# A recommender's cross-product tower on one core: tiles of 32 rows by 16 positions, lookups of four fields at once, and fifteen field pairs of the first layer multiplied out

## The reference, cut to what matters

```python
def _cin_layer(x0, xk, W, b):
    out = jnp.einsum('bhd,bmd,shm->bsd', xk, x0, W) + b[None, :, None]
    return jax.nn.relu(out)
e = jnp.stack([tbl_0[ids[:, 0]], ..., tbl_38[ids[:, 38]]], axis=1)   # (1024, 39, 16)
x1 = _cin_layer(e, e, W1, b1)        # W1 (128, 39, 39)
x2 = _cin_layer(e, x1, W2, b2)       # W2 (128, 128, 39)
z = jnp.concatenate([x1.sum(axis=-1), x2.sum(axis=-1)], axis=-1)
h = jnp.concatenate([z, dense_ctx], axis=1)
h = jnp.maximum(h @ W_top1 + b_top1, 0.0)
h = jnp.maximum(h @ W_top2 + b_top2, 0.0)
y = h @ W_top3
```

## Time and profile before

| | us |
|---|---|
| three runs | 1270.61, 1272.14, 1273.03 (median 1272.14) |
| the profiled execution | 1272.45 |
| its span, first to last instruction | 1270.7 |

### The profile page before, as it was taken

The page is one execution under the profiler, slowest core; times in us unless marked ns, Lnnn a source line. Parts: engine busy times, 40 slices in busy tenths (PEclk is TensorE's granted clock), DMA queues, the critical chain, the costliest instruction groups (busy, mean ns, idle before and its releaser), DMA issues.

```text
span 1270.7 us, 17332 instructions
## 1 busy us (share of the span) xinstructions
PE 1190.3 (94%) x4794; PEld 880.8 (69%) x4794; DVE 980.5 (77%) x3635; ACT 616.4 (49%) x1897; POOL 847.7 (67%) x788
## 2 busy tenths in 40 slices
PE   1279999999999999999999999999999999999996
PEld 0147777777777777777777667777777777776774
DVE  0118888888888888888888667888988888887695
ACT  2154555555545555555545444555555555554440
POOL 6788787777777777777778456877777544553450
PEclk9999999999999999999999999999999999999997
DMA  5000000000000000000000000000000000000000
GB/s 170 6 5 3 4 3 4 3 4 3 4 3 3 3 3 4 3 3 3 3 3 3 3 3 3 3 3 3 3 3 3 1 1 1 1 1 1 1 1 1
DMA packets 12837, 8.91 MB, mean 7 GB/s; under 512 B 6645, under 2 KB 12010, under 8 KB 12611
## 3 DMA queue, kind: packets, MB, share of 16 engines
q0 software_dynamic: 9984, 2.58, 2.4%
q1 hardware_dynamic: 2755, 5.22, 1.3%
HBM read 7.78 MB, written 0.00 MB: 6 GB/s over the span
## 4 chain that ended last, share of the span: by engine, by line
PE 82%; DVE 11%; POOL 3%; ACT 2%; issue 2%; DMA 0%; ACTq 0%; DVEq 0%
PE ps L592 20%; PE ps L594 19%; PE ps L593 19%; PE ps L572 15%; DVE acc L507 11%; PE ps L563 3%; POOL e L283 3%; PE ps L621 3%; ACT fy L374 1%; PE ps L551 1%; PE ps L668 0%; ACT z L396 0%; PE ps L659 0%; PE ps L658 0%; DMA e<-in_tbl,ids_sb 0%
## 5 line engine op out<-in xcount | busy, mean ns | idle before, releaser
L507 DVE SCALAR_TENSOR_TENSOR acc<-ps,e,acc 128x128 f32<-128x128 f32 x3200 | 854.1, 343 | 182.7 <-PE ps L594 179.3
L592 PE MATMUL ps<-w2h,x1h 128*128 128x512 f32 (+1 forms) x1280 | 591.6, 462 | 17.2 <-DVE acc L507 14.1
L292 POOL TENSOR_TENSOR fy<-fy 128x512 f32<-128x512 f32 (+1 forms) x256 | 401.3, 1568 | 284.2 <-ACT fy L374 264.7
L374 ACT ACTIVATE fy<-ps,e 128x128 f32<-128x128 f32 x1536 | 417.7, 387 | 253.3 <-PE ps L594 243.5
L594 PE MATMUL ps<-w2h,x1l 128*128 128x512 f32 (+1 forms) x1280 | 495.3, 387 | 0.0
L593 PE MATMUL ps<-w2l,x1h 128*128 128x512 f32 (+1 forms) x1280 | 494.0, 386 | 0.0
L283 POOL DMA_INDIRECT e<-in_tbl,ids_sb x312 | 302.9, 971 | 75.5 <-issue 51.4
L592 PEld LDWEIGHTS ps<-w2h,x1h 128*128 128x128 f32 x1280 | 240.6, 188 | 131.5 <-DVE acc L507 67.4
L593 PEld LDWEIGHTS ps<-w2l,x1h 128*128 128x128 f32 x1280 | 241.4, 189 | 89.9 <-issue 51.7
L594 PEld LDWEIGHTS ps<-w2h,x1l 128*128 128x128 f32 x1280 | 240.5, 188 | 48.8
L396 ACT ACTIVATE z<-ps 117x512 f32<-117x512 f32 x192 | 119.5, 623 | 181.5 <-PE ps L563 177.1
(11 more groups left out here) (57 smaller groups left out, 373.6 us busy)
## 6 DMA issues: line engine op xcount, KB each, us to landing
e<-in_tbl,ids_sb POOLq DMA_INDIRECT x312, 2.3
w_st<-in_w SPq DMA_DIRECT2D x1, 2496.0 KB, 13.2
wt_sb<-in_wt SPq DMA_DIRECT2D x2, 512.0 KB, 12.7
w_sb<-in_w1a SPq DMA_DIRECT2D x1, 409.5 KB
w1b_sb<-in_w1b SPq DMA_DIRECT2D x1, 409.5 KB
sel_st<-in_sel SPq DMA_DIRECT2D x1, 249.5 KB
ids_sb<-in_ids SPq DMA_DIRECT2D x1, 136.5 KB, 3.4
fold_sb<-in_fold SPq DMA_DIRECT2D x1, 124.8 KB
```

The lines of the kernel that those rows point to most:

```text
L292: nc.gpsimd.tensor_tensor(out, a, b, ALU.add).then_inc(s_fsum, 1)
L374: nc.scalar.activation(fy[:, p % 2, sub, m - MD, :], ps[:, 2 * (nth % RING) + sub, k * S:(k + 1) * S], ACT.Copy, scale=emb(p, sub, m)).the ...
L507: nc.vector.scalar_tensor_tensor(acc[:, sub, :] if m < MD - 1 else y, y, emb(p, sub, m), acc[:, sub, :] if m else fsum[:, p % 2, sub, :], ...
L592: nc.tensor.matmul(y, x1h[:, t % 2, at], w2h[:, cols], start=True, stop=False)
```

## The change

Three things are changed.

A tile is now 32 rows (BT) by all 16 positions, still 128 partitions by 4 and 512 columns: partition 32 q + r holds row r and the positions 4 q to 4 q + 3. All tables are joined to one, and a lookup fetches fields 4 j to 4 j + 3 of 32 rows: partition 32 k + r gets field 4 j + k. Ten lookups fill a tile, 320 in all, into `looked`, with four tiles in flight. DVE adds each table's first row to the ids at the start (`rows`). To bring `looked` to `e`, 16 small copies a tile are needed, from quarter k to quarter q of the partitions: eight on DVE (k = 0, 1) and eight on ACT (k = 2, 3), `put`. `high_part` and `low_part` now run for each tile.

Fifteen field pairs of the last shift are no longer made from squares: DVE multiplies them out (`products`, 128x60), they are split in two parts and go through `turn` together with the fields, which fills its 128 columns, and one product with the weights `wz` takes them in (`layer1_products`). The remaining 765 pairs fill six steps of 128 rows, where there were seven of 117.

The sum of p2 over the positions now runs over partitions too, so `sums` is a pair of products with a matrix of ones for each tile, and DVE's addition L530 is gone. `position_sum` has four additions for each tile where it had two or three.

The split of W2 moves from ACT and DVE to DVE alone, in two parts. `turn` moves from slot 4 to slot 10, the first step of layer 1 from slot 9 to slot 11, and the small network's steps to other slots.

```diff
+BT = 32
+Q = P // BT
-LOOKUPS_FIRST = 22
-LOOKUPS_PER_PAIR = 5
+LOOKUPS_FIRST = 3 * LOOKUPS
+LOOKUPS_PER_PAIR = LOOKUPS // 2
...
-    t, k = divmod(slot - 9, TILE_SLOTS)
+    t, k = divmod(slot - 11, TILE_SLOTS)
...
-    return t if p % 2 == 0 and s == 4 and t < TILES else None
+    return t if p % 2 == 1 and s == 0 and t < TILES else None
...
-    for c, s in enumerate((0, 6, 10, 14)):
+    for c, s in enumerate((0, 4, 14, 16)):
         MLP_AT[TILE_SLOTS * tile + s] = (g, 1, c)
-    for c, s in enumerate((0, 6)):
+    for c, s in enumerate((0, 4)):
...
+        def put_in_place(t, k, q):
+            n = len(range(k, M, Q))
+            return (e[q * BT:(q + 1) * BT, t, k:M:Q, :],
+                    looked[k * BT:(k + 1) * BT, t % LOOKED, 0:n, q * DT:(q + 1) * DT])
...
-                        e[:, i, m * D:(m + 1) * D], None, tables[m], bass.IndirectOffsetOnAxis(ids_sb[:, i, m:m + 1], 0)
-                    ).then_inc(s_look[i], 16)
+                        looked[:, t % LOOKED, j, :], None, table, bass.IndirectOffsetOnAxis(rows[:, t, j:j + 1], 0)
+                    ).then_inc(s_look[t], 16)
...
+                def put(t):
+                    act.wait_ge(s_look[t], 16 * LOOKUPS)
+                    for k in PUT_ACT:
+                        for q in range(Q):
+                            nc.scalar.activation(*put_in_place(t, k, q), ACT.Copy).then_inc(s_put_act, 1)
...
+                def put(t):
+                    dve.wait_ge(s_look[t], 16 * LOOKUPS)
+                    for k in PUT_DVE:
+                        for q in range(Q):
+                            nc.vector.tensor_copy(*put_in_place(t, k, q)).then_inc(s_put_dve, 1)
+                def products(t):
...
+                    nc.vector.tensor_tensor(prod[:, t % 2, :].rearrange("p (m d) -> p m d", d=DT), e[:, t, 0:ZP, :],
+                                            e[:, t, SHIFTS - 1:SHIFTS - 1 + ZP, :], ALU.mult).then_inc(s_prod, 1)
+                def split_w2(cols):
+
+                    nc.vector.tensor_scalar(w2h[:, cols], w2_st[:, cols], 0.5, None, ALU.mult).then_inc(s_w2h, 1)
+                    dve.wait_ge(s_w2h, 2 if cols.start == 0 else 1)
+                    nc.vector.scalar_tensor_tensor(w2l[:, cols], w2_st[:, cols], 0.5, w2h[:, cols], ALU.mult,
+                                                   ALU.subtract).then_inc(s_w2l, 1)
...
+                        filling = p % 2 == 0 and t < TILES
+                        if filling and j == 2:
+                            put(t)
+                        if p % 2 == 0 and j == 3 and t - 1 < TILES:
+                            first_layer_low(t - 1)
+                        if filling and j == 4:
+                            products(t)
+                        if filling and j == 5:
+                            low_part(t)
...
+                    nc.tensor.matmul(ps[:, BK_ACC1, :], wz[:], x0t[:, t % 2, :], start=True, stop=False)
...
+                    for sub in range(2):
+                        mm = nc.tensor.matmul(ps[:, BK_T, 0:BT], p2[:, t % 2, sub, :], rows_sum_sb[:], start=(sub == 0),
+                                              stop=(sub == 1))
```

More of the change, by code:

```diff
@@ L1 @@
+import itertools
 from contextlib import ExitStack
@@ L129, in staging_uses @@
 def staging_uses():
-    uses = [("turn", 0), ("turn", 1), ("expand", 0, C1 - 1)]
+    uses = [("turn", 0), ("turn", 1)]
     for p in range(PAIRS):
@@ L136, in staging_uses @@
                 uses.append(("turn", t))
-            if (i := block_step(p, s)) is not None:
-                uses.append(("sums", i))
+            if (t := sums_step(p, s)) is not None:
+                uses.append(("sums", t))
             if step := mlp_step(p, s):
                 uses.append(("mlp", *step))
-    uses.append(("sums", BLOCKS - 1))
+    uses.append(("sums", TILES - 1))
     return {use: n for n, use in enumerate(uses)}
@@ L344, in _ @@
                 first_fields(1)
-                n = M + LOOKUPS_FIRST
+                n = LOOKUPS_FIRST
                 for p in range(PAIRS):
-                    share = LOOKUPS_PER_PAIR + (p < 6)
+                    share = LOOKUPS_PER_PAIR
                     for j in range(1, A_BANKS):
                         step = share * j // A_BANKS - share * (j - 1) // A_BANKS
-                        for k in range(n, min(n + step, BLOCKS * M)):
+                        for k in range(n, min(n + step, TILES * LOOKUPS)):
                             look_up(k)
@@ L557, in expand @@
                         pe.wait_ge(s_x0t, t + 1)
-                    if t == 0 and v < C1 - 1:
-                        nc.tensor.matmul(ps[0:K1, v, :], sel_r[:, v, :], x0t[:, t % 2, :], start=True,
+                    if t == 0:
+                        nc.tensor.matmul(ps[:, v, :], sel_r[:, v, :], x0t[0:2 * M, t % 2, :], start=True,
                                          stop=True).then_inc(s_rep0, 1)
@@ L708 @@
     w1b[pp, kk] = w1[:, m[kk, pp], h[kk, pp]].T
-    w1a[LAST_ROWS, -1] = w1b[LAST_ROWS, -1] = x["L0_rec_b1"]
+    for row in (ZH, ZW, ZL):
+        for r in range(ZP):
+            w1a[row + r, C1], w1b[row + r, C1] = w1[:, r, SHIFTS - 1 + r], w1[:, SHIFTS - 1 + r, r]
+    w1a[[ONE_H, ONE_L], C1] = x["L0_rec_b1"]
     fold = np.zeros((K1, C1, M), np.float32)
@@ L726 @@
     }
[L727 removed]
     nc = bacc.Bacc("TRN2", target_bir_lowering=False, num_devices=1)
     data, aps = {}, {}
[L730 removed]
+    for name, a in {**arrays, "table": np.concatenate(tables)}.items():
         data[f"in_{name}"] = np.ascontiguousarray(a)
@@ L733 @@
     out = nc.dram_tensor("out_y", (B, 1), F32, kind="ExternalOutput").ap()
-    cin_tower(nc, [aps[f"tbl_{f}"] for f in range(M)], **{k: aps[k] for k in arrays},
-              out=out.rearrange("b o -> o b"))
+    cin_tower(nc, **aps, out=out.rearrange("b o -> o b"))
     r = run_bass_kernel_spmd(nc, [data], core_ids=[0])
```

325 lines of the change are left out of this document (188 added, 137 removed).

## The result

The changed kernel takes 1340.29 us (median of four runs, 1338.94 to 1340.87), the kernel before 1271.38 beside it (four runs): a ratio of 1.0541, 95% interval 1.0528 to 1.0554. Forecast were 1306 us and a range of 1247 to 1340. The direction was right, the size too small by 34 us, and the time lies 0.3 us above the range.

A forecast was written before the change was run, and what follows sets the result against it. PE was taken as the bound, with DVE work between slots 3 and 7 on its path. The sum 1272.45 - 35 - 12.6 - 15 + 105 - 8 - 1 = 1305.9 gave 1306 us, range 1247 to 1340.

The forecast's parts named there:

- What bounds the kernel: PE, busy 94%; DVE work between slots 3 and 7 of the even pair is on the path, elsewhere free.
- S: PE's new wait for DVE at slot 10: 0.15 + P + Q = 3.5 us a tile (2.5 to 4.8), +105 us.
- PE's own work: Each tile: one layer 1 step less (-1.10), `wz` +0.23, `sums` +0.45; sum -0.42 us, or -12.6 for 30 tiles.
- The old wait: PE's wait of some 0.5 us a tile at slot 9's expansion is taken out: -15 us for 30 tiles.
- P: DVE's eight copies, waiting for POOL's additions: 2.1 us (one wait) to 3.9 (second addition comes between), middle 3.0.
- Q: DVE's products: 0.2 us alone, up to 0.8 if they meet a POOL addition of slot 5; taken as 0.35.
- ScalarE's copies: ACT's eight copies in slot 4, at most 2.2 us, cost nothing while DVE is late; otherwise some 0.5 a tile.
- The small network: Four of its steps move to slot 4, into PE's waiting time: -8 us.
- The start: Fewer lookups ahead: layer 2 begins at 40 us, DVE's first field at 57 instead of 91.58; -35 us (-30 to -42).
- A: Rival: DVE's copies do not wait for POOL, S = 1.65; 1252 us (1240 to 1264), chance 0.20.
- B: Rival: POOL comes in between repeatedly and `turn`'s new place costs PE up to 1.6 us; S = 5.1, 1353 us, chance 0.15.
- C: Rival: two gains cancel, S near 2.3 with the copies' lower end and cheap products; 1270 to 1275 us, chance 0.03.

The follow-up runs named there:

- experiment 4: Changed kernel with DVE's copies and products behind slot 1 and ScalarE's copies in its slot 1: 1236.16 us, ratio 0.958 to the kernel before.
- experiment 7: Kernel before with six steps of layer 1 instead of seven, 78 products of pairs missing: 1255.94 us, ratio 0.971 to the kernel before.
- experiment 9: Changed kernel with all sixteen copies a tile on ScalarE, none on DVE: 1269.20 us, ratio 0.997 to the kernel before.
- experiment 8: Changed kernel with five steps of layer 1 instead of six, 125 pairs missing: 1356.60 us, ratio 1.049 to the kernel before, 1.010 to the changed kernel.
- experiment 1: Changed kernel with POOL's two additions in slot 2 of even pairs cut to one column of 128: 1276.21 us, ratio 0.989 to the kernel before.
- experiment 3: Changed kernel with DVE's copies behind slot 1 instead of slot 3, products left in place: 1259.98 us, ratio 0.977 to the kernel before.
- experiment 6: The kernel of experiment 4 with five steps of layer 1 instead of six, 125 pairs missing: 1231.09 us, ratio 0.967 to the kernel before.

## Why the prediction was right in its direction and wrong in its size

- **What bounds the kernel.** Right. Work on DVE between slots 3 and 7 was on the path, and the same work in slot 1 was nearly free (experiment 4: period 35.41, which is 0.76 above the 34.65 of the sum without S, where slot 3 cost 4.62).
- **PE's own work, -0.42 a tile.** Right. A step is worth 1.06 where PE is the bound (experiment 7), `wz` takes 0.23, the `sums` 0.36 (0.45 forecast).
- **The old wait, -15.** Right; the expansion has no wait ahead of it now.
- **The new wait, S = 3.5. This step failed.** Its mechanism is as described, though PE waits mostly ahead of slot 7 (2.98) and only then ahead of slot 10; x0t to x0t is 39.27 instead of 38.1. P, the time of the row of copies, had ends of 2.1 and 3.9, and I took the middle, 3.0. Measured are 3.91 (3.96, less the handover). The working for the upper end ("one slips in, POOL's second addition comes between, seven follow") is what happens, save that one more copy fits in between, which takes 0.2 off, and that the seventh copy meets a lookup, which puts 0.23 on; that the upper end comes out to 0.01 is luck. The middle was never one of the two cases: either POOL's next addition gets in or it doesn't, and a number between them describes no run. For the upper case spoke that POOL had the next addition queued, and that the earlier trace rows show POOL waiting only for one instruction's end, never for a row's. Q, the products, was taken as 0.35 and is 0.66 in 27 of 30 tiles, that is 0.58 with its handover: in 26 of them POOL's first addition of the sum over the positions, 0.73 long, is under way, not one of slot 5's as forecast. (The constant 0.15 is 6.95 less 6.85, more nearly 0.10.) S is then 0.15 + 3.91 + 0.58 = 4.64; the period gives 39.27 less 34.65, or 4.62. That lies within the bounds stated for S, 2.5 to 4.8, but the range of the time didn't follow them: with S = 4.8 the sum gives 1345, and the range ended at 1340.
- **ScalarE's copies, nothing.** Right for eight: 2.02 us, and no one waits. For sixteen it is 1.46 us (experiment 9).
- **The small network, -8.** Measured -7.3: its tiles lasted 20.5 and 11.8 us beyond the others before, 16.1 and 8.9 after.
- **The start, -35.** Right: first field 55.65 (forecast 57; 91.58 in the earlier trace rows), first product of layer 2 at 39.85 (40). The two lookups beside the split of W2 lasted 3.36 and 4.19 us. x1 of the second tile is made 35.3 us earlier.

With the measured terms the sum is 1272.45 - 35.3 - 12.6 - 15 + 139.2 - 7.3 - 1 = 1340.4, against 1340.5 for the profiled execution. That checks a tile as a whole and not its single terms: 12.6 and 15 weren't measured in the changed kernel. With the periods' 111 in place of these two and of S the sum is 1339.9. The miss is P, 0.91 x 30 = 27 us, and Q, 0.23 x 30 = 7.

One thing the sum hides is shown by experiment 8: with a wait this long, PE's terms don't add any more. DVE sets the stretch from 612.03 on, and work taken from PE inside it only lengthens PE's wait.

**The rivals.** A is refuted by the rows and by experiment 1. B was close in time (1353; S = 5.1) by another mechanism: POOL does come in between, but the expansion behind `turn` in slot 10 has its operands (PE starts it at 628.54 without a wait), and what PE waits for in slot 10 is DVE's bank (0.78). That B's time is nearer than the forecast's is luck. C is out.

## What to carry to other kernels

Where small instructions on one engine can be held by long ones on another, look at what the other has queued, and price each meeting as one case or another, not as a mean. Place such instructions ahead of the other engine's work, then look again at what follows them: an instruction that comes sooner can meet the next one (experiment 3). And a busy share of 96% doesn't say that less work on that engine shortens the kernel (experiment 6).

## What I had not expected of the hardware

**The granted clock falls behind a wait of 3 us.** In the changed kernel, in every second tile up to 660 us and in every tile from 870 to 1190; one of them:

```profile
579.00:581.00 2.00, 0.00 (x0) 0.00 (x0) 2.00 (x9) 0.30 (x2) 1.99 (x2) 1.00 0.09 8
581.00:583.00 2.00, 1.96 (x5) 1.57 (x6) 2.00 (x7) 0.00 (x0) 1.69 (x3) 0.50 0.00 0
584.40:586.00 1.60, 1.60 (x9) 1.38 (x9) 1.60 (x8) 0.44 (x3) 1.11 (x4) 0.99 0.00 0
```

PE idles to 581, then works at 0.50, 1.2 GHz, until 584.4. The tiles with such a stretch and those without are equally long, 39.2 to 39.3: without it PE waits 1.22 to 1.27 for DVE in slot 10, with it that wait is gone. With a wait of 3.84 the stretch doubles in two of three tiles, and these are 0.8 to 1.3 us longer (experiment 8). So a cut in PE's work lengthened the kernel by 1%.

**How DVE and POOL hand over.** In all 30 tiles of the loop the first copy ended just behind POOL's first addition, the second ran between the two, and the third waited for the second addition (1.17 to 1.20). The port pair that the two engines share is described as an exclusive lock in the Trainium skill, "SBUF — State Buffer", section "SBUF: two separate sides". The trace agrees for these copies: 1.26 and 1.20 us beside an addition, 0.17 beside none. It also shows that a row of copies doesn't keep POOL out: its second addition comes in between the members of the row. Who waits is decided a little behind POOL's recorded start, as the products show in two tiles:

```profile
622.73 0.92 POOL L352 TENSOR_TENSOR xs<-x 128x256 f32<-128x256 f32 x1
622.84 0.21 DVE L535 TENSOR_TENSOR prod<-e 128x60 f32<-128x60 f32 x1
...
661.45 0.73 POOL L352 TENSOR_TENSOR xs<-x 128x256 f32<-128x256 f32 x1
661.59 0.66 DVE L535 TENSOR_TENSOR prod<-e 128x60 f32<-128x60 f32 x1
```

Begun 0.11 us behind POOL's start, the products take 0.21 and POOL's addition is 0.19 longer; begun 0.14 behind it, they wait. In this trace all 88 copies and products that began 0.12 or more behind an addition's start, and before its end, ended 0.03 to 0.16 behind its end; the two that began sooner (0.08 and 0.11) did not wait. In the other trace of the changed kernel the line lies at 0.12 too: of two that began there one waited.
